# Two small products as one of 512 columns: reordering the LoRA part of a conditional residual kernel

## Chip, cores and metric

One core of a Trainium2 chip (trn2). The metric is the device time of one launch in microseconds, as a median of repeated runs.

## What is computed

For each of 8 batch elements, x is 512 tokens by 256 channels, fp32. Two residual layers follow each other. The first layer's weights are a mixture of 8 experts under one mask, by the element's 8 conditions; the second has a base matrix and 8 LoRA experts of rank 16, mixed by the same conditions:

```
# first layer
masked_w = weight * mask[None, :, :]
w_bot = jnp.einsum('bg,got->bot', y, masked_w)
x = x + jnp.einsum('bnt,bot->bno', x, w_bot) + bias
# second layer, scaling 2
out = jnp.einsum('btc,oc->bto', x, W_base) + b_base
h = jnp.einsum('btc,erc->bter', x, As)
lora = jnp.einsum('bter,eor,be->bto', h, Bs, w)
x = x + out + lora * SCALING
```

## The kernel before

The kernel folds both layers and both residuals into one 256x256 matrix per element: M = W0 W1, where W0 is identity plus the mixed and masked weights and W1 is identity plus base plus LoRA product. The output is M applied to x, plus a bias. All fp32 products are made of three matmuls of split operands: hi x hi, hi x lo and lo x hi, where `_hi` is a value rounded to fp32r and `_lo` what is left of it. So every operand has to be split, by two engines one behind the other: ScalarE writes `_hi` by a copy, then VectorE or GpSimd writes `_lo` by a subtraction.

The order is written out by hand, engine by engine, with semaphores between. On TensorE it is:

- 28 warm-up matmuls, then the LoRA products of elements 0 and 1 (`lora_first`).
- Mask products: `mixed(q)` for the 8 packs q = 0..7, each 4 matmuls of 128 columns. Pack q gives 32 of the 256 columns of the mixed weights of all 8 elements. They go to four PSUM banks in turn (`ps_mix`, which are the `ps_out` banks), so pack q from 4 on waits until VectorE took out pack q - 4. VectorE's `w0(q)` takes a pack out of PSUM, times the mask, into W0 and counts `w0_done`.
- LoRA products of elements 2 and 3 (`lora(b)`) between the mask products. `lora(b)` is two groups of three matmuls of 256 columns into bank b % 2 of `ps_lora`, and waits until VectorE took element b - 2 out. VectorE's `w1(b)` adds the base to it, giving W1 of the element.
- The first halves of the merges of elements 0 and 1, the LoRA products of 4 and 5 as a pair (`lora_pair`: 6 matmuls of 512 columns, bank j for row half j of both elements), then the second halves.
- For each element: merge of the next one, then apply (12 matmuls of 512 columns) of this one. The LoRA pair of 6 and 7 stands behind the third apply.

The first merges are split in halves so that they can start before all packs are in. Their first half needs a chain of its own: GpSimd splits W1 of element 0 (`w1_lo(0)`, line 191, after ScalarE's `w1_hi(0)`, line 240), adds the identity to the first half of W0 of elements 0 and 1 when four packs are in (line 206, `eye_first`), splits W1 of element 1, and, after ScalarE's `_hi` of W0 (line 286, `ramp_hi`), writes W0_lo of the first halves (line 210, `ramp_first`). In `merge_half`, this last is what the third of the three matmul pairs waits for (line 463), while line 580 holds the group until W1_lo is there. The second halves do the same by VectorE (lines 410 and 383) and ScalarE (line 295). `SINGLE` says how many elements have their LoRA product one at a time; waits on `lora_mm` and `w1_done` count by it. `W1BUF = 4` buffers hold W1.

GpSimd's order around the change is `w1_lo(0)`, identity, `w1_lo(1)`, W0_lo of the first halves, `w1_lo(2)`, and then a wait for VectorE's `x_lo` of element 0.

Of the kernel before, what the change touches and what calls it, by code (L numbers as in the profile page):

```python
# [5 lines left out]
def conditional_residual_kernel(nc: bass.Bass, head: bass.AP, rest: bass.AP, packs: bass.AP, factors_A: bass.AP,  # L6
# [10 lines left out]
    P = 128  # L17
    NB, _, XW = xT.shape
    NT = 2
# [9 lines left out]
    EXPW = KQ * C  # L29
    PACKW = EXPW + NT * TQ  # L30
    SCALING = 32.0 / 16
    SINGLE = 4
    XBUF = 4
    W1BUF = 4
    WARM = 28
# [5 lines left out]
    with ExitStack() as ctx:  # L41
# [40 lines left out]
        A_hi = sb("A_hi", [P, C], f32r)  # L82
        A_lo = sb("A_lo", [P, C], f32r)
        B_hi = sb("B_hi", [P, NB, C], f32r)
        B_lo = sb("B_lo", [P, NB, C], f32r)
# [20 lines left out]
        ps_lora = [pb(f"ps_lora{i}", [P, NT, C]) for i in range(2)]  # L106
# [17 lines left out]
        row_done, bias_mm, bias_done, bhi_done, blo_done = sem("row_done"), sem("bias_mm"), sem("bias_done"), sem("bhi_done"), sem("blo_done")  # L124
# [104 lines left out]
        @block.scalar  # L229
        def _(act):  # L230
            def b_hi(b):
                nc.scalar.activation(B_hi[:, b], B_er, ACT.Copy,
                                     scale=cond_er[:, b:b + 1]).then_inc(bhi_done, 1)

            def w1_hi(b):
                act.wait_ge(w1_done, b + 1 if b < SINGLE else b // 2 * 2 + 2)

                if b >= W1BUF:
                    act.wait_ge(merge_mm, b - W1BUF + 1)
                nc.scalar.activation(W1_hi[:, b % W1BUF], W1[:, b % W1BUF], ACT.Copy).then_inc(w1hi_done, 1)  # L240

            def w0_hi(b):

                act.wait_ge(eye_done, b - 1)
                act.wait_ge(merge_mm, b - 1)
                nc.scalar.activation(W0_hi[:, b % 2], W0[:, b], ACT.Copy).then_inc(w0hi_done, 1)  # L246

            def m_hi(b):
                act.wait_ge(merge_mm, b + 1)

                if b >= 2:
                    act.wait_ge(apply_mm, 2 * (b - 1))
                nc.scalar.activation(M_hi[:, b % 2], ps_merge[b % 2][:, :, :], ACT.Copy).then_inc(mhi_done, 1)  # L253

            def split_x_hi(b):
                act.wait_ge(x_in[b], 16)

                if b >= XBUF:
                    act.wait_ge(apply_mm, 2 * (b - XBUF + 1))
                nc.scalar.activation(x_hi[:, b % XBUF], x_sb[:, b], ACT.Copy).then_inc(xhi_done, 1)  # L260

            def out0(b):
                act.wait_ge(apply_mm, 2 * b + 1)
                if b == 0:
                    act.wait_ge(bias_done, 1)

                if b >= 2:
                    act.wait_ge(stored[b % 2][0], 16 * (b // 2))
                nc.scalar.activation(out_sb[:, b % 2, 0, :], ps_out[b % 2 * NT][:, :], ACT.Identity,  # L269
                                     bias=bias_sb[:, 0, b:b + 1]).then_inc(out_done[0], 1)  # L270

            act.dma_start(lora_sb[:, OBT:OBT + C], factors_B).then_inc(B_arrived, 16)

            act.wait_ge(warm_set, 1)
            nc.scalar.activation(table_sb[:, :], warm[:, 0:1], ACT.Copy)
            act.dma_start(base_sb[:, :, :], base.rearrange("p (j o) -> p j o", j=NT)).then_inc(base_in, 16)

            act.wait_ge(B_arrived, 16)
            act.wait_ge(lora_arrived, 16)
            for b in range(NB):  # L280
                b_hi(b)
            w1_hi(0)
            w1_hi(1)

            act.wait_ge(eye_first, 1)
            nc.scalar.activation(W0_hi[:, 0:2, :, 0:H], W0[:, 0:2, :, 0:H], ACT.Copy).then_inc(ramp_hi, 1)
            w1_hi(2)
            split_x_hi(0)

            act.wait_ge(rows_in, 16)  # L290
            act.wait_ge(w0_done, NQ)
            nc.scalar.activation(ps_row, bias0_row, ACT.Copy).then_inc(row_done, 1)
            for b in range(2):
                act.wait_ge(eye_second, 1)
                nc.scalar.activation(W0_hi[:, b, :, H:C], W0[:, b, :, H:C], ACT.Copy).then_inc(ramp_hi, 1)
            w1_hi(3)
            m_hi(0)
            split_x_hi(1)
            w0_hi(2)
            m_hi(1)  # L300
            for b in range(NB):
                if b + 3 < NB:
                    w0_hi(b + 3)
                if b + 2 < NB:
                    split_x_hi(b + 2)
                if 4 <= b + 3 < NB:
                    w1_hi(b + 3)
                if b + 2 < NB:
                    m_hi(b + 2)
                out0(b)  # L310

            b = NB - 1
            act.wait_ge(apply_mm, 2 * b + 2)
            act.wait_ge(stored[b % 2][1], 16 * (b // 2))
            nc.scalar.activation(out_sb[:, b % 2, 1, 0:TOK // 2], ps_out[b % 2 * NT + 1][:, 0:TOK // 2], ACT.Identity,
                                 bias=bias_sb[:, 1, b:b + 1]).then_inc(last_done, 1)

        @block.vector
        def _(dve):
# [8 lines left out]
            def w1(b):  # L328
                dve.wait_ge(lora_mm, b + 1)
                nc.vector.tensor_tensor(W1[:, b], ps_lora[b % 2][:, :, :], base_sb[:, :, :],  # L330
                                        ALU.add).then_inc(w1_done, 1)

            def w1_pair(b):
                dve.wait_ge(lora_mm, SINGLE + (b - SINGLE) // 2 + 1)
                dve.wait_ge(w1lo_done, b - W1BUF + 2)
                at = b % W1BUF
                for j in range(NT):
                    nc.vector.tensor_tensor(W1[:, at:at + 2, j, :], ps_lora[j][:, :, :],
                                            base_sb[:, j, :].unsqueeze(1).to_broadcast([P, 2, C]),
                                            ALU.add).then_inc(w1_done, 1)  # L340

            def w0(q):
                dve.wait_ge(mix_mm, q + 1)

                dve.wait_ge(pack_in[q], 16)
                ts = slice(q * TQ, (q + 1) * TQ)
                nc.vector.tensor_tensor(  # L347
                    W0[:, :, :, ts].rearrange("p b j t -> p j b t"),
                    ps_mix[q % 4][:, :].rearrange("p (j b t) -> p j b t", j=NT, t=TQ),
                    pack(q)[1].unsqueeze(2).to_broadcast([P, NT, NB, TQ]),  # L350
                    ALU.mult).then_inc(w0_done, 1)
# [43 lines left out]
            dve.wait_ge(fixed_done, 1)  # L395
            w0(0)
            w0(1)
            dve.wait_ge(base_done, NT)
            w1(0)
            w0(2)  # L400
            w1(1)
            w0(3)
            w0(4)
            w1(2)
            w0(5)
            w0(6)
            w1(3)
            w0(7)
            dve.wait_ge(w0_done, NQ)
            nc.vector.tensor_tensor(W0[:, 0:2, 1, H:C], W0[:, 0:2, 1, H:C], ident[:, :].unsqueeze(1).to_broadcast([P, 2, P]),  # L410
# [41 lines left out]
        def _(pe):  # L452
            def product(out, terms, lo_ready=None, mid_ready=None):


                for n, (hi_l, _, hi_r, _) in enumerate(terms):
                    nc.tensor.matmul(out, hi_l, hi_r, start=(n == 0), stop=False)  # L457
                if mid_ready is not None:
                    pe.wait_ge(*mid_ready)
                for hi_l, _, _, lo_r in terms:  # L460
                    nc.tensor.matmul(out, hi_l, lo_r, start=False, stop=False)  # L461
                if lo_ready is not None:
                    pe.wait_ge(*lo_ready)
                for n, (_, lo_l, hi_r, _) in enumerate(terms):
                    mm = nc.tensor.matmul(out, lo_l, hi_r, start=False, stop=(n == len(terms) - 1))  # L465
                return mm
# [23 lines left out]
                term(1, 1, A_lo, B_hi)  # L490
                term(1, 1, A_hi, B_lo, last=True).then_inc(lora_mm, 1)

            def lora(b):

                pe.wait_ge(blo_done, b + 1)
                pe.wait_ge(w1_done, b - 1)
                for j in range(NT):
                    cols = slice(j * P, (j + 1) * P)
                    mm = product(ps_lora[b % 2][:, j, :],
                                 [(A_hi[:, cols], A_lo[:, cols], B_hi[:, b], B_lo[:, b])])  # L500
                mm.then_inc(lora_mm, 1)

            def lora_pair(b):

                pe.wait_ge(blo_done, b + 2)
                pe.wait_ge(w1_done, b)
                both = slice(b, b + 2)
                for j in range(NT):
                    cols = slice(j * P, (j + 1) * P)
                    mm = product(ps_lora[j][:, :, :], [(A_hi[:, cols], A_lo[:, cols], B_hi[:, both], B_lo[:, both])])  # L510
                mm.then_inc(lora_mm, 1)
# [57 lines left out]
            lora_first()  # L569
            for q in range(4):  # L570
                mixed(q)
            lora(2)
            mixed(4)
            mixed(5)
            lora(3)
            mixed(6)
            mixed(7)
            for b in range(2):
# [75 lines left out]
```

## Time and profile before

| what | value |
|---|---|
| median of 3 runs | 56.79 us (56.75 to 57.19) |
| the profiled execution | 56.88 us |
| its span | 55.1 us |
| TensorE busy (matmuls) | 50.7 us, 92% |
| VectorE, ScalarE, GpSimd busy | 39.5, 31.7, 31.5 us |

The span runs from the first to the last instruction that the profile shows; the rest of the execution's time lies around it. PE is TensorE, PEld its weight loads, DVE VectorE, ACT ScalarE, POOL GpSimd. In a timeline a row gives the start, the duration of the whole group, the engine, line and operation, what it writes and reads, and in brackets the idle time of the engine before it with what ended it. Matmuls overlap: the next one starts before the one in front has ended, so TensorE's pace is read from start to start. Buffer numbers and the digits of W0 and W1 are left out in the names: W stands for both.

### The profile page before, as it was taken

The numbers are of one execution on the slowest core, as the hardware profiler recorded it, in microseconds if no ns is written. First come the engines' busy times: TensorE is split into PE (matmuls) and PEld (weight loads), VectorE is DVE, ScalarE is ACT, GpSimd is POOL, SyncE is SP. The second block draws the span as 40 slices with busy tenths as digits, with TensorE's granted clock in tenths as the row PEclk, the third lists the DMA queues.
The fourth block names the chain that finished last, engine by engine and source line by source line (L and its number), as shares of the span: only waits on it lengthen the run. The fifth ranks groups of instructions, "written<-read, shape, count | busy, mean of one in ns | idle before, by whom it ended". The sixth has DMA issues, their size and how long they took to land.

```text
span 55.1 us, 972 instructions
## 1 busy us (share of the span) xinstructions
PE 50.7 (92%) x330; PEld 45.6 (83%) x330; DVE 39.5 (72%) x64; ACT 31.7 (58%) x53; POOL 31.5 (57%) x30
## 2 busy tenths in 40 slices
PE   2998999699999999999999999999999999999900
PEld 2988999699998978998898889889889889888800
DVE  0049999989596975999999988689929809805030
ACT  1939900447809499619705992992992950850800
POOL 4003400199990098999995999999999910000000
PEclk9999999999999999999999999999999999999999
DMA  0599999999999995000630072063054054059582
GB/s 0 136 377 313 363 390 400 426 401 426 425 384 413 416 396 208 15 0 0 253 134 0 12 272 109 0 241 146 0 223 158 0 205 176 0 196 372 193 286 95
DMA packets 5477, 11.79 MB, mean 214 GB/s; under 512 B 609, under 2 KB 1377, under 8 KB 5473
## 3 DMA queue, kind: packets, MB, share of 16 engines
q1 hardware_dynamic: 5184, 11.35, 54.7%
q10 hardware_dynamic: 288, 0.39, 2.1%
q8 instruction: 2, 0.03, 0.2%
q14 instruction: 3, 0.02, 0.1%
HBM read 7.54 MB, written 4.19 MB: 213 GB/s over the span
## 4 chain that ended last, share of the span: by engine, by line
PE 77%; DVE 11%; DMA 5%; issue 2%; DVEq 0%
PE ps_out L457 13%; PE ps_out L461 13%; PE ps_out L465 13%; PE ps_merge L457 7%; PE ps_merge L461 7%; PE ps_merge L465 7%; DVE B_lo L324 7%; PE ps_out L527 6%; DMA lora_sb<-factors_A_dram 5%; PE ps_lora L457 3%; PE ps_lora L461 3%; PE ps_lora L465 3%; DVE W L330 1%; DVE out_sb L448 1%; DVE A_lo L389 1%
## 5 line engine op out<-in xcount | busy, mean ns | idle before, releaser
L191 POOL TENSOR_TENSOR W_lo<-W,W_hi 128x512 fp32r<-128x512 f32 x8 | 13.3, 1657 | 5.3 <-ACT W_hi L240 5.3
L358 DVE TENSOR_TENSOR x_lo<-x_sb,x_hi 128x1024 fp32r<-128x1024 f32 x8 | 11.9, 1485 | 0.2 <-ACT x_hi L260 0.2
L457 PE MATMUL ps_out<-x_hi,M_hi 128*128 128x512 f32 (+1 forms) x32 | 9.8, 388 | 0.0
L461 PE MATMUL ps_out<-x_lo,M_hi 128*128 128x512 f32 (+1 forms) x32 | 9.7, 384 | 0.0
L465 PE MATMUL ps_out<-x_hi,M_lo 128*128 128x512 f32 (+1 forms) x32 | 9.7, 383 | 0.0
L253 ACT ACTIVATE M_hi<-ps_merge 128x512 fp32r<-128x512 f32 x8 | 4.8, 595 | 7.6 <-PE ps_merge L465 7.6
L197 POOL TENSOR_TENSOR W_lo<-W,W_hi 128x512 fp32r<-128x512 f32 x6 | 8.8, 1459 | 0.3 <-ACT W_hi L246 0.3
L260 ACT ACTIVATE x_hi<-x_sb 128x1024 fp32r<-128x1024 f32 x8 | 8.4, 1055 | 0.0
L240 ACT ACTIVATE W_hi<-W 128x512 fp32r<-128x512 f32 x8 | 5.0, 629 | 5.9 <-DVE W L330 3.6
L373 DVE TENSOR_SCALAR out_sb<-ps_out,bias_sb 128x512 f32<-128x512 f32 x7 | 5.2, 747 | 4.1 <-PE ps_out L465 4.0
L201 POOL TENSOR_TENSOR W<-W,ident 128x256 f32<-128x256 f32 x6 | 6.4, 1071 | 2.9 <-DVE x_lo L358 2.9
L527 PE MATMUL ps_out<-packs_sb 128*128 128x128 f32 x64 | 7.6, 275 | 0.0
L527 PEld LDWEIGHTS ps_out<-packs_sb 128*128 128x128 f32 x64 | 7.4, 192 | 0.0
L461 PEld LDWEIGHTS ps_out<-x_lo,M_hi 128*128 128x128 f32 x32 | 5.9, 188 | 1.2
L465 PEld LDWEIGHTS ps_out<-x_hi,M_lo 128*128 128x128 f32 x32 | 5.9, 188 | 1.2
L365 DVE TENSOR_TENSOR M_lo<-ps_merge,M_hi 128x512 fp32r<-128x512 f32 x8 | 5.5, 687 | 2.0 <-ACT M_hi L253 1.9
L269 ACT ACTIVATE out_sb<-ps_out,bias_sb 128x512 f32<-128x512 f32 x8 | 5.5, 684 | 2.2 <-PE ps_out L465 2.2
L457 PE MATMUL ps_merge<-W_hi 128*128 128x256 f32 x32 | 6.6, 288 | 0.0
L461 PE MATMUL ps_merge<-W_lo,W_hi 128*128 128x256 f32 x32 | 6.4, 283 | 0.0
L465 PE MATMUL ps_merge<-W_hi,W_lo 128*128 128x256 f32 x32 | 6.4, 283 | 0.0
L457 PEld LDWEIGHTS ps_out<-x_hi,M_hi 128*128 128x128 f32 x32 | 5.5, 189 | 0.9 <-issue 0.2
L347 DVE TENSOR_TENSOR W<-ps_out,packs_sb 128x512 f32<-128x512 f32 x8 | 5.4, 686 | 0.9 <-PE ps_out L527 0.8
(58 smaller groups left out, 71.4 us busy)
## 6 DMA issues: line engine op xcount, KB each, us to landing
x_sb<-xT_dram SPq DMA_DIRECT2D x8, 512.0 KB, 10.5
outT_dram<-out_sb SPq DMA_DIRECT2D x15, 256.0 KB, 2.3
packs_sb<-packs_dram SPq DMA_DIRECT2D x7, 288.0 KB, 5.4
rows_sb<-rows_dram SPq DMA_DIRECT2D x1, 384.0 KB, 7.1
base_sb<-base_dram ACTq DMA_DIRECT2D x1, 256.0 KB, 3.6
outT_dram<-out_sb SPq DMA_DIRECT2D x2, 128.0 KB, 1.8
packs_sb<-head_dram SPq DMA_DIRECT2D x1, 192.0 KB, 3.5
packs_sb<-rest_dram SPq DMA_DIRECT2D x1, 160.0 KB, 3.9
```

The lines of the kernel that those rows point to most:

```text
L191: pool.tensor_tensor(W1_lo[:, b % W1BUF], W1[:, b % W1BUF], W1_hi[:, b % W1BUF].bitcast(f32), ALU.subtract).then_inc(w1lo_done, 1)
L197: pool.tensor_tensor(W0_lo[:, b % 2], W0[:, b], W0_hi[:, b % 2].bitcast(f32), ALU.subtract).then_inc(w0lo_done, 1)
L201: pool.tensor_tensor(diagonal(b), diagonal(b), ident[:, :].unsqueeze(1).to_broadcast([P, NT, P]), ALU.add).then_inc(eye_done, 1)
L260: nc.scalar.activation(x_hi[:, b % XBUF], x_sb[:, b], ACT.Copy).then_inc(xhi_done, 1)
L269: nc.scalar.activation(out_sb[:, b % 2, 0, :], ps_out[b % 2 * NT][:, :], ACT.Identity, bias=bias_sb[:, 0, b:b + 1]).then_inc(out_done[0], 1)
L347: nc.vector.tensor_tensor(W0[:, :, :, ts].rearrange("p b j t -> p j b t"), ps_mix[q % 4][:, :].rearrange("p (j b t) -> p j b t", j=NT, t=T ...
L358: nc.vector.tensor_tensor(x_lo[:, b % XBUF], x_sb[:, b], x_hi[:, b % XBUF].bitcast(f32), ALU.subtract).then_inc(xlo_done, 1)
L365: nc.vector.tensor_tensor(M_lo[:, b % 2], ps_merge[b % 2][:, :, :], M_hi[:, b % 2].bitcast(f32), ALU.subtract).then_inc(mlo_done, 1)
L457: nc.tensor.matmul(out, hi_l, hi_r, start=(n == 0), stop=False)
L461: nc.tensor.matmul(out, hi_l, lo_r, start=False, stop=False)
L465: mm = nc.tensor.matmul(out, lo_l, hi_r, start=False, stop=(n == len(terms) - 1))
L527: mm = nc.tensor.matmul(dst[:, j, :, k, :], pack(q)[0][:, k, j * P:(j + 1) * P], mix, start=True, stop=True)
```

## The change

The LoRA products of elements 2 and 3 are made as a pair of 512 columns, behind the sixth mask product (pack 5) where the first of them stood behind the fourth. VectorE takes W1 of elements 0 and 1 behind three mask products, the first of them one place later than before, and W1 of 2 and 3 in the broadcast form of `w1_pair`, behind W0 of pack 5. ScalarE splits x of element 0 ahead of W1 of element 2. `lora(b)` is gone.

```
--- before.py
+++ after.py
@@ -29,7 +29,7 @@
     EXPW = KQ * C
     PACKW = EXPW + NT * TQ
     SCALING = 32.0 / 16
-    SINGLE = 4
+    SINGLE = 2
     XBUF = 4
     W1BUF = 4
     WARM = 28
@@ -284,8 +284,8 @@
 
             act.wait_ge(eye_first, 1)
             nc.scalar.activation(W0_hi[:, 0:2, :, 0:H], W0[:, 0:2, :, 0:H], ACT.Copy).then_inc(ramp_hi, 1)
+            split_x_hi(0)
             w1_hi(2)
-            split_x_hi(0)
 
             act.wait_ge(rows_in, 16)
             act.wait_ge(w0_done, NQ)
@@ -332,7 +332,8 @@
 
             def w1_pair(b):
                 dve.wait_ge(lora_mm, SINGLE + (b - SINGLE) // 2 + 1)
-                dve.wait_ge(w1lo_done, b - W1BUF + 2)
+                if b >= W1BUF:
+                    dve.wait_ge(w1lo_done, b - W1BUF + 2)
                 at = b % W1BUF
                 for j in range(NT):
                     nc.vector.tensor_tensor(W1[:, at:at + 2, j, :], ps_lora[j][:, :, :],
@@ -395,16 +396,15 @@
             dve.wait_ge(fixed_done, 1)
             w0(0)
             w0(1)
+            w0(2)
             dve.wait_ge(base_done, NT)
             w1(0)
-            w0(2)
             w1(1)
             w0(3)
             w0(4)
-            w1(2)
             w0(5)
+            w1_pair(2)
             w0(6)
-            w1(3)
             w0(7)
             dve.wait_ge(w0_done, NQ)
             nc.vector.tensor_tensor(W0[:, 0:2, 1, H:C], W0[:, 0:2, 1, H:C], ident[:, :].unsqueeze(1).to_broadcast([P, 2, P]),
@@ -490,16 +490,6 @@
                 term(1, 1, A_lo, B_hi)
                 term(1, 1, A_hi, B_lo, last=True).then_inc(lora_mm, 1)
 
-            def lora(b):
-
-                pe.wait_ge(blo_done, b + 1)
-                pe.wait_ge(w1_done, b - 1)
-                for j in range(NT):
-                    cols = slice(j * P, (j + 1) * P)
-                    mm = product(ps_lora[b % 2][:, j, :],
-                                 [(A_hi[:, cols], A_lo[:, cols], B_hi[:, b], B_lo[:, b])])
-                mm.then_inc(lora_mm, 1)
-
             def lora_pair(b):
 
                 pe.wait_ge(blo_done, b + 2)
@@ -569,10 +559,9 @@
             lora_first()
             for q in range(4):
                 mixed(q)
-            lora(2)
             mixed(4)
             mixed(5)
-            lora(3)
+            lora_pair(2)
             mixed(6)
             mixed(7)
             for b in range(2):
```

VectorE, from its first mask product taken out to the identity add on the second halves (the order of before, then the order now; W0 rows are mask packs 0 to 7, W1 rows LoRA elements):

```order
L347 TENSOR_TENSOR W0<-ps_out0,packs_sb 128x2x8x32
L347 TENSOR_TENSOR W0<-ps_out1,packs_sb 128x2x8x32
L330 TENSOR_TENSOR W1<-ps_lora0,base_sb 128x512
L347 TENSOR_TENSOR W0<-ps_out2,packs_sb 128x2x8x32
L330 TENSOR_TENSOR W1<-ps_lora1,base_sb 128x512
L347 TENSOR_TENSOR W0<-ps_out3,packs_sb 128x2x8x32
L347 TENSOR_TENSOR W0<-ps_out0,packs_sb 128x2x8x32
L330 TENSOR_TENSOR W1<-ps_lora0,base_sb 128x512
L347 TENSOR_TENSOR W0<-ps_out1,packs_sb 128x2x8x32
L347 TENSOR_TENSOR W0<-ps_out2,packs_sb 128x2x8x32
L330 TENSOR_TENSOR W1<-ps_lora1,base_sb 128x512
L347 TENSOR_TENSOR W0<-ps_out3,packs_sb 128x2x8x32
```

Now, on the same engine and over the same place:

```order
L348 TENSOR_TENSOR W0<-ps_out0,packs_sb 128x2x8x32
L348 TENSOR_TENSOR W0<-ps_out1,packs_sb 128x2x8x32
L348 TENSOR_TENSOR W0<-ps_out2,packs_sb 128x2x8x32
L330 TENSOR_TENSOR W1<-ps_lora0,base_sb 128x512
L330 TENSOR_TENSOR W1<-ps_lora1,base_sb 128x512
L348 TENSOR_TENSOR W0<-ps_out3,packs_sb 128x2x8x32
L348 TENSOR_TENSOR W0<-ps_out0,packs_sb 128x2x8x32
L348 TENSOR_TENSOR W0<-ps_out1,packs_sb 128x2x8x32
L339 TENSOR_TENSOR W1<-ps_lora0,base_sb 128x2x256
L339 TENSOR_TENSOR W1<-ps_lora1,base_sb 128x2x256
L348 TENSOR_TENSOR W0<-ps_out2,packs_sb 128x2x8x32
L348 TENSOR_TENSOR W0<-ps_out3,packs_sb 128x2x8x32
```

W1 of element 0 went from third to fourth place, W1 of element 1 stayed fifth; the two of elements 2 and 3 stand together, and the last two packs follow them.

TensorE, from the mask product of pack 3 to the first merge, before (bank names tell the pack and the element):

```order
L527 MATMUL ps_out3<-packs_sb 128x8x16 x4
L457 MATMUL ps_lora0<-B_hi,A_hi 128x256
L461 MATMUL ps_lora0<-B_lo,A_hi 128x256
L465 MATMUL ps_lora0<-B_hi,A_lo 128x256
L457 MATMUL ps_lora0<-B_hi,A_hi 128x256
L461 MATMUL ps_lora0<-B_lo,A_hi 128x256
L465 MATMUL ps_lora0<-B_hi,A_lo 128x256
L527 MATMUL ps_out0<-packs_sb 128x8x16 x4
L527 MATMUL ps_out1<-packs_sb 128x8x16 x4
```

And TensorE now, from the same product on:

```order
L517 MATMUL ps_out3<-packs_sb 128x8x16 x4
L517 MATMUL ps_out0<-packs_sb 128x8x16 x4
L517 MATMUL ps_out1<-packs_sb 128x8x16 x4
L457 MATMUL ps_lora0<-B_hi,A_hi 128x512
L461 MATMUL ps_lora0<-B_lo,A_hi 128x512
L465 MATMUL ps_lora0<-B_hi,A_lo 128x512
L457 MATMUL ps_lora1<-B_hi,A_hi 128x512
L461 MATMUL ps_lora1<-B_lo,A_hi 128x512
L465 MATMUL ps_lora1<-B_hi,A_lo 128x512
L517 MATMUL ps_out2<-packs_sb 128x8x16 x4
```

The mask products of packs 4 and 5 moved ahead of the LoRA products, and the group that stood between packs 5 and 6 (the other six of 256 columns) is now part of the pair there.

## Rows read from the trace of the kernel before

**Rows 1.** The page: busy time, granted clock, chain that ended last.

```profile
PE 50.7 (92%) x330; PEld 45.6 (83%) x330; DVE 39.5 (72%) x64; ACT 31.7 (58%) x53; POOL 31.5 (57%) x30
...
PEclk9999999999999999999999999999999999999999
...
PE 77%; DVE 11%; DMA 5%; issue 2%; DVEq 0%
```

**Rows 2.** Timeline of PE; start us, us, engine, line, operation [idle before].

```profile
5.96 3.73 PE L527 MATMUL ps_out<-packs_sb 128*128 128x128 f32 x32
10.15 0.36 PE L457 MATMUL ps_lora<-B_hi,A_hi 128*128 128x256 f32 x1 [0.45 <-DVE W L330]
...
10.94 1.95 PE L527 MATMUL ps_out<-packs_sb 128*128 128x128 f32 x16
...
13.44 1.95 PE L527 MATMUL ps_out<-packs_sb 128*128 128x128 f32 x16
15.13 0.48 PE L457 MATMUL ps_merge<-W_hi 128*128 128x256 f32 x2
...
15.69 0.40 PE L465 MATMUL ps_merge<-W_hi,W_lo 128*128 128x256 f32 x2
...
16.65 0.40 PE L457 MATMUL ps_lora<-B_hi,A_hi 128*128 128x512 f32 x1
...
18.04 0.40 PE L457 MATMUL ps_merge<-W_hi 128*128 128x256 f32 x2
```

**Rows 3.** Timeline of DVE, 8.1 to 16.9 us.

```profile
8.12 1.29 DVE L347 TENSOR_TENSOR W<-ps_out,packs_sb 128x512 f32<-128x512 f32 x2
9.32 0.68 DVE L330 TENSOR_TENSOR W<-ps_lora,base_sb 128x512 f32<-128x512 f32 x1
9.92 0.68 DVE L347 TENSOR_TENSOR W<-ps_out,packs_sb 128x512 f32<-128x512 f32 x1
10.52 0.68 DVE L330 TENSOR_TENSOR W<-ps_lora,base_sb 128x512 f32<-128x512 f32 x1
11.11 0.68 DVE L347 TENSOR_TENSOR W<-ps_out,packs_sb 128x512 f32<-128x512 f32 x1
...
15.73 0.68 DVE L347 TENSOR_TENSOR W<-ps_out,packs_sb 128x512 f32<-128x512 f32 x1
16.45 0.43 DVE L410 TENSOR_TENSOR W<-W,ident 128x256 f32<-128x256 f32 x1
```

**Rows 4.** Timeline of ACT, 10 to 15 us.

```profile
10.04 0.63 ACT L240 ACTIVATE W_hi<-W 128x512 fp32r<-128x512 f32 x1 [3.02 <-DVE W L330]
...
12.74 0.63 ACT L286 ACTIVATE W_hi<-W 128x512 fp32r<-128x512 f32 x1 [0.88 <-POOL W L206]
...
13.89 1.04 ACT L260 ACTIVATE x_hi<-x_sb 128x1024 fp32r<-128x1024 f32 x1
```

**Rows 5.** Timeline of POOL, 10.7 to 15.2 us.

```profile
10.75 1.28 POOL L191 TENSOR_TENSOR W_lo<-W,W_hi 128x512 fp32r<-128x512 f32 x1 [4.60 <-ACT W_hi L240]
11.98 0.73 POOL L206 TENSOR_TENSOR W<-W,ident 128x256 f32<-128x256 f32 x1
12.67 1.30 POOL L191 TENSOR_TENSOR W_lo<-W,W_hi 128x512 fp32r<-128x512 f32 x1
13.92 1.28 POOL L210 TENSOR_TENSOR W_lo<-W,W_hi 128x512 fp32r<-128x512 f32 x1
```

**Rows 6.** Timelines of POOL, then DVE, where the two meet later.

```profile
25.29 1.30 POOL L197 TENSOR_TENSOR W_lo<-W,W_hi 128x512 fp32r<-128x512 f32 x1
...
28.24 1.30 POOL L197 TENSOR_TENSOR W_lo<-W,W_hi 128x512 fp32r<-128x512 f32 x1
30.22 2.20 POOL L191 TENSOR_TENSOR W_lo<-W,W_hi 128x512 fp32r<-128x512 f32 x1 [0.68 <-ACT W_hi L240]
...
25.50 2.18 DVE L358 TENSOR_TENSOR x_lo<-x_sb,x_hi 128x1024 fp32r<-128x1024 f32 x1
...
28.20 1.27 DVE L338 TENSOR_TENSOR W<-ps_lora,base_sb 128x512 f32<-128x512 f32 x2
```

More of the change, by code:

```diff
@@ L31, in conditional_residual_kernel @@
     SCALING = 32.0 / 16
-    SINGLE = 4
+    SINGLE = 2
     XBUF = 4
@@ L286, in _ @@
             nc.scalar.activation(W0_hi[:, 0:2, :, 0:H], W0[:, 0:2, :, 0:H], ACT.Copy).then_inc(ramp_hi, 1)
+            split_x_hi(0)
             w1_hi(2)
-            split_x_hi(0)
             act.wait_ge(rows_in, 16)
@@ L334, in w1_pair @@
                 dve.wait_ge(lora_mm, SINGLE + (b - SINGLE) // 2 + 1)
-                dve.wait_ge(w1lo_done, b - W1BUF + 2)
+                if b >= W1BUF:
+                    dve.wait_ge(w1lo_done, b - W1BUF + 2)
                 at = b % W1BUF
@@ L397, in _ @@
             w0(1)
+            w0(2)
             dve.wait_ge(base_done, NT)
             w1(0)
-            w0(2)
             w1(1)
@@ L403, in _ @@
             w0(4)
-            w1(2)
             w0(5)
+            w1_pair(2)
             w0(6)
-            w1(3)
             w0(7)
@@ L491, in lora_first @@
                 term(1, 1, A_hi, B_lo, last=True).then_inc(lora_mm, 1)
[L493 to L501, printed above, removed]
             def lora_pair(b):
@@ L571, in _ @@
                 mixed(q)
-            lora(2)
             mixed(4)
             mixed(5)
-            lora(3)
+            lora_pair(2)
             mixed(6)
```

## The prediction

> **What bounds the kernel now.** I read the page first. TensorE is busy for 50.7 of 55.1 us, its granted clock is at 9 (full, the 2.4 GHz level) in every slice, and the chain that ended last is TensorE for 77%, with VectorE at 11% ahead of it [rows 1]. So only two things can move the end: a pause of TensorE, or the number and length of its instructions. The next view is TensorE's own timeline [rows 2]. The reader is to see one pause behind the mask products: those of packs 0 to 3 end at 9.69 (5.96 + 3.73), and the third LoRA product starts at 10.15, 0.46 later, released by VectorE's W1. From there on it goes from one group to the next. VectorE's timeline [rows 3] says why: W1 of element 0 runs from 9.32 to 10.00, and the LoRA product follows 0.14 later (rounded starts and ends; every sum here is good to some 0.02).
>
> Then I look for what stands just behind TensorE, since a pause that goes only pays up to the next thing that is late. That is the first half of the first two merges. It starts at 15.13 and its third pair of matmuls (W0_lo) at 15.69 [rows 2]. Its inputs come by a second chain: VectorE W1(0) [rows 3], ScalarE W1_hi(0) at 10.04 [rows 4], then four GpSimd instructions: W1_lo(0) at 10.75, identity into W0 at 11.98, W1_lo(1) at 12.67, and W0_lo of the first halves from 13.92 to 15.20 [rows 5]. The first of them waits for ScalarE, the other three have no idle time noted before them. So GpSimd is a full chain of 4.45 us from 10.75 to 15.20, and is only 0.49 us ahead of TensorE's use at 15.69. That margin decides this case.
>
> **The change part by part.**
>
> 1. *TensorE's LoRA products.* Removed: 12 matmuls of 256 columns in two groups; the first takes 0.79 from its start to the next group (10.15 to 10.94) [rows 2]. Added: 6 of 512 columns. The same shape runs at 16.65, and its six take 1.39 (to 18.04) [rows 2]. Behind mask products the first matmul costs some 0.07 more (0.79 for six where six of the 0.12 pitch would be 0.72), so 1.46 against 2 x 0.79 = 1.58: a gain of 0.12 on TensorE's own time.
>
> 2. *The pause at 9.69 goes, since the mask products of packs 4 and 5 now follow at once.* Mask products go at (3.73 - 0.28) / 31 = 0.111 each, so packs 0 to 3 give way at 5.96 + 32 x 0.111 = 9.52. They need W0 of packs 0 and 1 taken out (VectorE is done with both at 9.41 [rows 3]) and packs 4 and 5 landed; the DMA view bounds that poorly, but this term is shown below to have 0.9 us of cover. Sixteen mask products take 15.13 - 13.44 = 1.69 [rows 2], which gives 11.21. The pair then waits for W1 of elements 0 and 1. VectorE writes the second at 10.52 to 11.20 in both kernels, plus the 0.14: 11.34. Six matmuls: 12.80. Packs 6 and 7: 14.49. TensorE so reaches the merges 0.64 ahead of the 15.13 of before, and the W0_lo pair, 0.56 further on, at 15.05 in place of 15.69.
>
> 3. *VectorE takes W0 of pack 2 ahead of W1(0).* The pitch is 0.60 (9.32, 9.92, 10.52) [rows 3]. The product of pack 2 is finished at 5.96 + 23 x 0.111 + 0.28 = 8.8, so this instruction starts at 9.32 without a wait, and W1(0) runs at 9.92 to 10.60: 0.60 later. W1(1) stays at 10.52 and W0 of pack 3 at 11.11, as five instructions stand ahead of the latter either way.
>
> 4. *What waits behind W1(0).* ScalarE's W1_hi(0) is the head of its queue, so it moves from 10.04 to 10.64. GpSimd's W1_lo(0) moves from 10.75 to 11.35. By the same pitches the other three go to 12.58, 13.27 and 14.52, and W0_lo ends at 15.80. Their other inputs come no later: the identity wants four W0 (11.11 + 0.68 = 11.79), W1_lo(1) wants W1_hi(1) (from 11.20, a 0.63 instruction), and W0_lo wants ScalarE's W0_hi, which moves with the identity from 12.74 to 13.34 and ends at 13.97, well ahead of 14.52 [rows 4]. So this chain is 0.60 late, and its margin was 0.49. TensorE gets there at 15.05, waits until 15.80, and starts at 15.94 if the step from GpSimd costs what VectorE's did, 0.14. Against 15.69 that is **+0.25 us**. The trace has no case of TensorE waiting for GpSimd. The nearest steps are 0.04 (W1 to ScalarE, 10.00 to 10.04) and 0.14 to 0.21 (VectorE to TensorE, with the slow first matmul of 0.07), so the term lies between +0.15 and +0.32; I take 0.14 since it is the same waiting engine.
>
> 5. *W1 of elements 2 and 3 in two broadcast instructions.* Same number, and the same form costs 1.27 for two at 28.20 [rows 6] where the old ones were 0.68 each. They are ready at 12.96 and run from 13.02; W0 of pack 6 then starts at 14.22 and of pack 7 at 14.82, where it was 15.73. The identity add on VectorE comes at 15.54 in place of 16.45 [rows 3]. Cost nothing: TensorE wants the second halves of W0_hi and W0_lo only from 18.04 [rows 2]. Likewise W1_hi(2) behind x_hi(0) on ScalarE: x has landed by 13.89 [rows 4], ScalarE gets there at 13.97, and W1_lo(2) is first used in the third merge, after 22 us. If that cover went, a late x would hold up W1_hi(2) and the bias row, which TensorE needs for none of the first merges. The second LoRA pair, at 16.65, wants W1 of elements 2 and 3, done by 14.3.
>
> 6. *GpSimd beside VectorE.* Now VectorE's identity add (15.54, two operands in SBUF) meets the last 0.26 us of GpSimd's W0_lo (to 15.80). Such a meeting stands in the trace: GpSimd started at 25.29 and took 1.30, its usual time, while VectorE's x_lo, issued at 25.50, took 2.18 [rows 6]. The one that came second paid. So W0_lo keeps 15.80 and VectorE's add ends at 15.80 + 0.43 = 16.23, still ahead of the 16.88 of before. Were the meeting shared out instead, W0_lo could lose up to the add's 0.43 and the time would be 57.47. The Trainium skill (SBUF — State Buffer, SBUF: two separate sides) says that a VectorE instruction with two SBUF inputs and a GpSimd instruction take one shared port pair as an exclusive lock, the first to start holding it for its whole length; by that rule GpSimd's chain isn't touched and the sum stays, and the rows at 25.29 and 25.50 agree.
>
> The sum: TensorE's 0.12 and the 0.46 pause are gained ahead of 15 us and handed back as a new wait of 0.89 (15.05 to 15.94). What is left is +0.25. Behind the merges TensorE has no wait that could take this up again, and ScalarE, VectorE and GpSimd are released there by TensorE's merges, so they move along. Span 55.10 + 0.25 = 55.35, and the profiled execution 56.88 + 0.25 = 57.13. The median of the three runs before stands 0.09 below the profiled one, so the forecast is 56.79 + 0.25 = **57.04 us**. What measurement can tell here is about 1%, 0.57 us.
>
> **The rivals.**
>
> A, *the head start is kept.* If GpSimd's chain doesn't hold TensorE, it comes 0.64 early: 56.15. For it: spans on GpSimd are rough, and TensorE never waited there before. Against: three of four instructions stand back to back, and VectorE's order makes the head of the chain 0.60 late whatever its end is. To keep half of the gain W0_lo would have had to be done by 14.6, 0.6 ahead of its record.
>
> B, *a wash.* If GpSimd's real end lies 0.2 ahead of its record, the shift is about +0.05: 56.84. This is still within 1%.
>
> C, *slower.* One of GpSimd's four instructions, W1_lo(1) or W0_lo, at 13.27 to 15.80, is caught by VectorE and takes the long form, 2.20 as at 30.22 where it met an x_lo, not 1.28 [rows 5, 6]: 0.92 more, 57.96. It decides from about 0.32 us of such delay on. For it: VectorE now runs the broadcast form at 13.02 to 14.22, which stood there never before. Against: the same form at 28.20 ran beside a GpSimd instruction of 1.30 at 28.24 [rows 6], and it has one operand in PSUM as all others in that stretch have. By the rule of the Trainium skill named above, with only one SBUF input it takes no lock, and C would not occur.
>
> D, *the change doesn't do what it says*, the LoRA pair waiting elsewhere. The printed orders speak against it, and its own cover is 0.9 us: packs late by that much change nothing.
>
> **How the numbers follow.** My forecast (with +0.15 to +0.32) has 0.75, B 0.10, A 0.04, C or the shared meeting 0.08 (of which half falls short of 1%), D and the rest 0.03. The range is 56.6 to 57.5: below, B and 0.24 more, about half the spread of 0.44 of the three times before; above, the shared meeting. A and C stay outside. Faster by over 1%: A and little else, 0.04. Slower by over 1%, beyond 57.36: part of C and of the step's upper bound, 0.08. Within 1%: 0.88.
>
> **What would show it.** In the profile after: no idle time of TensorE at 9.7; W1(0) on VectorE at 9.92; GpSimd's W0_lo from 14.5 to 15.8; idle time of 0.9 us on TensorE before the first W0_lo matmul, released by GpSimd; first product of the first apply 0.25 later than before. It is wrong if that wait is absent or under 0.6, if W1(0) isn't 0.6 late, if a GpSimd instruction in that stretch takes over 1.5 us, or if the clock row falls after the pause.

## The result and the profile after

The changed kernel takes 57.09 us (median of 10 runs, 57.02 to 57.53) where the kernel before takes 56.82 beside it: ratio 1.0053, 95% interval 1.003 to 1.0077. Forecast were +0.25 us and 57.04 us; measured are +0.27 us and 57.09 us. It is a small loss: its interval lies above no change, and its size inside the 1% that the prediction took as what measurement can tell.

The first profile of the changed kernel (one execution of 57.36 us, span 55.6) answers to [rows 2] to [rows 5], but not at the times forecast. TensorE's timeline, columns as in [rows 2]:

```profile
4.99 0.41 PE L471 MATMUL ps_lora<-B_hi,A_lo 128*128 128x256 f32 x1
5.20 0.41 PE L471 MATMUL ps_lora<-B_lo,A_hi 128*128 128x256 f32 x1
...
6.66 2.62 PE L517 MATMUL ps_out<-packs_sb 128*128 128x128 f32 x22
...
11.93 0.48 PE L457 MATMUL ps_lora<-B_hi,A_hi 128*128 128x512 f32 x1
...
15.11 0.48 PE L457 MATMUL ps_merge<-W_hi 128*128 128x256 f32 x2
...
16.09 0.50 PE L465 MATMUL ps_merge<-W_hi,W_lo 128*128 128x256 f32 x2 [0.27 <-POOL W_lo L210]
16.43 0.40 PE L457 MATMUL ps_merge<-W_hi 128*128 128x256 f32 x2
```

The kernel before, in the same place of TensorE's timeline:

```profile
5.01 0.28 PE L471 MATMUL ps_lora<-B_lo,A_hi 128*128 128x256 f32 x1
5.12 0.28 PE L471 MATMUL ps_lora<-B_hi,A_hi 128*128 128x256 f32 x1
```

VectorE's timeline of the changed kernel's execution:

```profile
9.53 0.69 DVE L348 TENSOR_TENSOR W<-ps_out,packs_sb 128x512 f32<-128x512 f32 x1 [0.20 <-PE ps_out L517]
10.14 1.28 DVE L330 TENSOR_TENSOR W<-ps_lora,base_sb 128x512 f32<-128x512 f32 x2
...
16.12 1.44 DVE L410 TENSOR_TENSOR W<-W,ident 128x256 f32<-128x256 f32 x1
```

And GpSimd's:

```profile
11.56 1.29 POOL L191 TENSOR_TENSOR W_lo<-W,W_hi 128x512 fp32r<-128x512 f32 x1 [4.39 <-ACT W_hi L240]
12.81 0.74 POOL L206 TENSOR_TENSOR W<-W,ident 128x256 f32<-128x256 f32 x1
13.52 1.27 POOL L191 TENSOR_TENSOR W_lo<-W,W_hi 128x512 fp32r<-128x512 f32 x1
14.75 1.29 POOL L210 TENSOR_TENSOR W_lo<-W,W_hi 128x512 fp32r<-128x512 f32 x1
15.99 1.29 POOL L191 TENSOR_TENSOR W_lo<-W,W_hi 128x512 fp32r<-128x512 f32 x1
```

The signs that were forecast are there: no idle time of TensorE at 9.7, and a new one before the first W0_lo product, released by GpSimd's line 210. But TensorE is late. In the LoRA products at its head one matmul follows the other every 0.21 us (4.99, 5.20), where it was some 0.12 before (5.01, 5.12); below this distance from start to start is called the pitch. The mask products begin at 6.66, not at 5.96 [rows 2]. (The x22 of their row is where that view ends; all go on to 11.93.) So TensorE idles only 0.27 at the merges, and VectorE's W0 of pack 2 has to wait 0.20 for its mask product. The prediction had named an idle time under 0.6 as a sign that it is wrong, and this profile shows that sign. Whether the late TensorE belongs to the change is the question of the eighth experiment.

### The profile page after: what moved, and what is told of

Its sections match the earlier page's. It is cut to its first block, busy times and chain, and to the rows that moved or that the text cites. A ratio compares the mean times of both kernels' runs of the same rounds, so it can differ in the third digit from the quotient of the medians.

```text
span 55.6 us, 959 instructions
## 1 busy us (share of the span) xinstructions
PE 51.5 (93%) x324; PEld 46.1 (83%) x324; DVE 40.8 (74%) x64; ACT 31.6 (57%) x53; POOL 31.5 (57%) x30
## 4 chain that ended last, share of the span: by engine, by line
PE 81%; POOL 8%; DVE 2%; issue 2%; ACT 1%; DVEq 0%
PE ps_out L457 13%; PE ps_out L461 13%; PE ps_out L465 13%; PE ps_merge L465 7%; PE ps_merge L457 7%; PE ps_merge L461 6%; PE ps_merge L558 6%; PE ps_out L517 5%; PE ps_lora L471 5%; POOL W_lo L191 5%; POOL W_lo L210 2%; PE ps_lora L457 2%; PE ps_lora L465 2%; PE ps_lora L461 2%; POOL W L206 1%
## 5 line engine op out<-in xcount | busy, mean ns | idle before, releaser
L457 PEld LDWEIGHTS ps_merge<-W_hi 128*128 128x128 f32 x32 | 5.2, 190 | 0.6
```

## The experiments

Theory: TensorE's head start is real, but the first W0_lo product waits for GpSimd's chain, whose head W1(0) the change made 0.60 later. Rivals: the LoRA pair and its place cost the time; or VectorE's order costs nothing. The first four ran together, then the next four, then three, each group beside runs of the kernel before. e10 and e11 are single profiled executions and so not in the table; "the ramp" is all that stands ahead of the first apply.

| kernel | median us | before beside it | ratio (95% interval) |
|---|---|---|---|
| e1 W1(0) back | 56.73 | 56.85 | 0.9979 (0.9949 to 1.0008) |
| e2 VectorE's order alone | 57.43 | 56.85 | 1.0087 (1.0062 to 1.0113) |
| e3 GpSimd +0.6, before | 57.07 | 56.85 | 1.0041 (1.0024 to 1.0059) |
| e4 GpSimd +0.6, changed | 57.65 | 56.85 | 1.0127 (1.0103 to 1.0152) |
| e5 identity on VectorE | 56.88 | 56.84 | 1.0003 (0.9972 to 1.0033) |
| e6 ScalarE's order undone | 57.18 | 56.84 | 1.0066 (1.0037 to 1.0094) |
| e7 place without pair | 56.54 | 56.84 | 0.9961 (0.9929 to 0.9992) |
| e8 changed kernel again | 57.14 | 56.84 | 1.0064 (1.0029 to 1.0098) |
| e9 as e7, again | 56.68 | 56.86 | 0.9968 (0.9942 to 0.9994) |

**e1, from the changed kernel.**

```
-            w0(2)
             dve.wait_ge(base_done, NT)
             w1(0)
+            w0(2)
             w1(1)
```

> The changed kernel with one line moved: VectorE takes W1 of element 0 behind two mask packs again, as before the change; the LoRA pair stays. Theory (GpSimd's chain, whose head is W1(0), holds the first W0_lo product): W1(0) ends at about 10.0, W0_lo on GpSimd at about 15.2, TensorE reaches its use early, at about 15.05, and starts it at about 15.3, 0.35 earlier than in the kernel before (15.69). Time 56.82 - 0.35 = 56.47 us, 0.6 below the changed kernel. Rival (the pair and its place cost the time): no gain from the line, 57.1 us.

The line alone takes the loss away: 56.73 is 0.36 below the changed kernel's 57.09. The quickest five executions of twelve lie at 56.47 to 56.53, at the forecast; the others go up to 57.47. The interval of e1 still touches no change against the kernel before. Its profile came from an execution of 56.95 us, with the pitch of 0.21: W0_lo on GpSimd ends at 13.83 + 1.30 = 15.13, and TensorE, which came to it only at 15.64, doesn't wait:

```profile
6.64 5.52 PE L517 MATMUL ps_out<-packs_sb 128*128 128x128 f32 x48
...
15.64 0.40 PE L465 MATMUL ps_merge<-W_hi,W_lo 128*128 128x256 f32 x2
```

In this execution the limit has changed sides: GpSimd is done 0.51 ahead of TensorE's use. The wait of under 0.3 that the theory has for the quick executions was not seen, as the second profile of this kernel (e11, 56.90 us) had the pitch of 0.21 once more.

> The kernel with W1(0) behind two packs and the pair kept, once more, for a profile with the pitch of 0.12. Theory: GpSimd's W0_lo ends at 15.1 to 15.2 and TensorE starts its product 0.05 later with a wait of under 0.3 us; time 56.5 us. Rival: TensorE waits at the mask packs before, and not for GpSimd.

**e2, from the kernel before:** the reverse of e1's edit, with single LoRA products.

> The kernel before with only VectorE's order changed: W0 of pack 2 ahead of W1(0), LoRA products one by one as before. Theory: W1(0) is 0.60 later, the third LoRA product waits until 10.75 in place of 10.15, and everything of TensorE behind it goes 0.60 later: 57.4 us; GpSimd's chain (0.60 later too, with 0.49 to spare) is then hidden behind TensorE's own delay. Rival (the order on VectorE costs nothing): 56.8 us. So the LoRA pair would be worth 0.3 us in the changed kernel.

57.43 against 57.4 forecast. The third LoRA product starts at 10.85, 0.70 later than in the kernel before, released by VectorE's W1:

```profile
10.85 0.36 PE L457 MATMUL ps_lora<-B_hi,A_hi 128*128 128x256 f32 x1 [0.58 <-DVE W L330]
```

VectorE's order costs 0.6 us by itself, and the rest of the change (the new place of the LoRA products, and the pair) gives 0.3 of it back.

**e3 and e4: a dose for GpSimd,** in the kernel before and in the changed one.

```
             w1_lo(0)
+            pool.tensor_tensor(spare[:, :, :], ident[:, :].unsqueeze(1).to_broadcast([P, 2, P]),
+                               ident[:, :].unsqueeze(1).to_broadcast([P, 2, P]), ALU.add)
             pool.wait_ge(w0_done, NQ // 2)
```

(The line that makes the unused tile `spare` is left out.)

> The kernel before with one extra GpSimd instruction of 256 columns (0.7 us, into an unused tile) behind the split of W1(0). Theory: the chain had 0.49 less the step of 0.04 to 0.14 to spare, so of 0.70 some 0.3 shows: 57.15 us. Rival (GpSimd had ample room): 56.8 us.

> The changed kernel with the same extra GpSimd instruction of 0.7 us. Theory: the chain is what TensorE waits for, so all of it shows: 57.1 + 0.7 = 57.8 us. Rival (the loss is elsewhere and GpSimd's wait is hidden): under 57.4 us.

The instruction moved its successor by 0.57 us (12.41 to 12.98 in e4). The kernel before lost 0.22 and the changed one 0.56 (57.65 against 57.09, which ran in another group). So the changed kernel has no room left on GpSimd, and the one before had some 0.35. e4's profile shows the wait at its full size and the step from GpSimd to TensorE, 14.92 + 1.28 = 16.20 to 16.25:

```profile
14.43 0.50 PE L460 MATMUL ps_merge<-W_hi 128*128 128x256 f32 x2
14.77 0.40 PE L464 MATMUL ps_merge<-W_lo,W_hi 128*128 128x256 f32 x2
16.25 0.50 PE L468 MATMUL ps_merge<-W_hi,W_lo 128*128 128x256 f32 x2 [1.07 <-POOL W_lo L213]
```

and on GpSimd's timeline:

```profile
14.92 1.28 POOL L213 TENSOR_TENSOR W_lo<-W,W_hi 128x512 fp32r<-128x512 f32 x1
```

**e6: the changed kernel with `w1_hi(2)` ahead of `split_x_hi(0)` again.**

> The changed kernel with ScalarE's order put back: W1 of element 2 ahead of x of element 0. ScalarE then waits for the pair's W1 until 14.3 and does x_hi(0) behind it, up to 1 us later. Theory (ScalarE's order costs and gains nothing, as its outputs are first used after 17 us): 57.1 us, as the changed kernel. Rival (the swap was a part of the result): over 57.3 us, if TensorE's second merge halves or x come late.

57.18 us and a ratio of 1.0066, against 1.0064 of e8 beside it: no effect. Its profile (57.10 us) is the cleanest view of what was forecast, as its LoRA matmuls have the pitch of 0.12:

```profile
5.90 5.63 PE L517 MATMUL ps_out<-packs_sb 128*128 128x128 f32 x48
11.29 0.47 PE L457 MATMUL ps_lora<-B_hi,A_hi 128*128 128x512 f32 x1
...
14.46 0.48 PE L457 MATMUL ps_merge<-W_hi 128*128 128x256 f32 x2
14.78 0.40 PE L461 MATMUL ps_merge<-W_lo,W_hi 128*128 128x256 f32 x2
15.81 0.51 PE L465 MATMUL ps_merge<-W_hi,W_lo 128*128 128x256 f32 x2 [0.63 <-POOL W_lo L210]
16.15 0.40 PE L457 MATMUL ps_merge<-W_hi 128*128 128x256 f32 x2
```

and GpSimd's instruction that it waits for:

```profile
14.47 1.29 POOL L210 TENSOR_TENSOR W_lo<-W,W_hi 128x512 fp32r<-128x512 f32 x1
```

**e7 and e9: the kernel before with the place alone.** LoRA products stay single; W1(0) stays behind two packs.

```
-            lora(2)
             mixed(4)
             mixed(5)
+            lora(2)
             lora(3)
...
             w0(4)
-            w1(2)
             w0(5)
-            w0(6)
+            w1(2)
             w1(3)
+            w0(6)
             w0(7)
```

> The kernel before with both later LoRA products moved behind the mask product of pack 5, but still one by one with 256 columns, and VectorE's W1 of elements 0 and 1 in their old places. Theory: the place removes the pause and GpSimd's chain stays the limit, so the time is that of the first experiment, 56.5 to 56.7 us; the broadcast pair form itself is worth at most 0.1. Rival (the 512-column form is what gains): 56.8 us or more.

> The kernel that keeps single LoRA products, both behind pack 5, once more, since its interval touched that of no change. Theory: it beats the kernel before in executions whose first LoRA matmuls have the pitch of 0.12, by 0.3 us (56.5), and not in those with 0.21, where TensorE itself comes 0.6 late; median 56.6 us. Rival (the gain was chance): 56.8 us.

In both groups it is faster than the kernel before, by 0.30 and 0.18 us (0.4% and 0.3%), with both intervals below 1. This is the version that beats both kernels. It is no slower than e1, so the 512-column form isn't what gains. The two profiles show what the pitch does here. e9's, of 56.64 us, has five matmuls at 0.21. TensorE comes to the W0_lo product 0.21 earlier than in the kernel before and finds it ready:

```profile
6.44 5.52 PE L527 MATMUL ps_out<-packs_sb 128*128 128x128 f32 x48
...
15.48 0.40 PE L465 MATMUL ps_merge<-W_hi,W_lo 128*128 128x256 f32 x2
```

as GpSimd's part ends at 13.95 + 1.28 = 15.23:

```profile
13.95 1.28 POOL L210 TENSOR_TENSOR W_lo<-W,W_hi 128x512 fp32r<-128x512 f32 x1
```

e7's, of 57.18 us, has some eleven matmuls at 0.21: the mask products begin at 6.94 and the W0_lo product at 15.99, 0.30 later than in the kernel before, and the execution is 0.30 us longer than the profiled one of before. So e9's theory (no gain where the pitch is 0.21) was right for e7's execution and wrong for e9's own: how many matmuls are slow decides.

**e8: the changed kernel once more.**

> The changed kernel itself, for a second look. In its first profile the first seven LoRA matmuls had a pitch of 0.21 us and the mask products began at 6.66; in the kernel before it was 0.12 and 5.96. Theory: in an execution with the pitch of 0.12 TensorE reaches the first W0_lo product at about 15.0 and waits until about 15.8 to 15.9; in one with 0.21 it comes at 15.6 and waits until 16.1. Time 57.1 us. Rival (the 0.6 us later arrival at 15.6 belongs to the change): the arrival stays at 15.6 with the pitch of 0.12 too.

57.14 us. In its profile (57.08 us) three matmuls have the pitch of 0.21 and the mask products begin at 6.17. TensorE comes to the merges at 14.61 and so to the product at about 15.17, and GpSimd lets it go at 15.77:

```profile
6.17 5.52 PE L517 MATMUL ps_out<-packs_sb 128*128 128x128 f32 x48
...
14.61 0.48 PE L457 MATMUL ps_merge<-W_hi 128*128 128x256 f32 x2
...
15.77 0.50 PE L465 MATMUL ps_merge<-W_hi,W_lo 128*128 128x256 f32 x2 [0.44 <-POOL W_lo L210]
16.11 0.40 PE L457 MATMUL ps_merge<-W_hi 128*128 128x256 f32 x2
```

So the late arrival of the first profile wasn't the change's: it goes with the number of slow LoRA matmuls at the head. The profile of the kernel before with e3's dose had some ten of them, and its mask products began at 6.78. The idle time is again under the prediction's 0.6; from start to start the wait is 15.77 - 15.17 = 0.60.

**e5 and e10: from e1, the identity add (`eye_first`) taken from GpSimd and given to VectorE behind `w0(3)`.**

```
             w1_lo(0)
-            pool.wait_ge(w0_done, NQ // 2)
-            pool.tensor_tensor(W0[:, 0:2, 0, 0:H], W0[:, 0:2, 0, 0:H], ident[:, :].unsqueeze(1).to_broadcast([P, 2, P]),
-                               ALU.add).then_inc(eye_first, 1)
             w1_lo(1)
...
             w0(3)
+            dve.wait_ge(w0_done, NQ // 2)
+            nc.vector.tensor_tensor(W0[:, 0:2, 0, 0:H], W0[:, 0:2, 0, 0:H], ident[:, :].unsqueeze(1).to_broadcast([P, 2, P]),
+                                    ALU.add).then_inc(eye_first, 1)
             w0(4)
```

> The kernel of the first experiment (W1(0) behind two packs, LoRA pair kept) with the identity add on the first halves of W0 moved from GpSimd to VectorE, behind W0 of pack 3. Theory: GpSimd's chain loses one of its four links (0.7 us), less what VectorE's add takes from it while both want SBUF (up to 0.4), so W0_lo ends at about 14.85 and TensorE, at its use at about 15.03, no longer waits: 0.64 ahead of the kernel before, 56.2 us, 0.2 to 0.3 below the first experiment's quick executions. VectorE's own later work moves by up to 0.7 us and has that room. Rival (the first experiment's W0_lo wasn't the last to come any more, or VectorE's delay of W1 of elements 2 and 3 decides): 56.5 us or more.

> The kernel with the identity add on VectorE once more, for a profile of an execution with the pitch of 0.12, since its time (56.7 at best) missed the 56.2 that was expected. Theory: VectorE's add, issued at about 11.6, is held by GpSimd's W1_lo(0) until 11.94 and, if GpSimd's next one then comes first, until 13.2; the packs and the pair's W1 behind it on VectorE come up to 1.2 us late and TensorE waits there. Rival: TensorE waits for mask packs to land, at 8 to 11 us, in any kernel that wants them earlier, and the add has no part in it.

56.88 us (56.66 at best), where 56.2 was expected: a miss. e5's own profile (57.25 us) has the pitch of 0.21 for some eleven matmuls; e10's (56.72 us) has the short pitch. There the first part went as forecast: the W0_lo product starts at 15.09 without a wait, 0.60 earlier than before, and the first apply at 19.16, 0.49 earlier. Neither the theory of e10 nor its rival holds: VectorE's add took 0.47 at 11.76, held up by almost nothing. Most of the lead is lost at the fifth merge (element 4). TensorE's timeline of e10:

```profile
31.71 0.39 PE L461 MATMUL ps_lora<-B_lo,A_hi 128*128 128x512 f32 x1
31.94 0.39 PE L465 MATMUL ps_lora<-B_hi,A_lo 128*128 128x512 f32 x1
32.38 0.47 PE L457 MATMUL ps_merge<-W_hi 128*128 128x256 f32 x2
```

and GpSimd's:

```profile
28.09 1.29 POOL L197 TENSOR_TENSOR W_lo<-W,W_hi 128x512 fp32r<-128x512 f32 x1
30.07 2.21 POOL L191 TENSOR_TENSOR W_lo<-W,W_hi 128x512 fp32r<-128x512 f32 x1 [0.69 <-ACT W_hi L237]
```

The pitch of 0.23 becomes 0.44 ahead of that merge. It waits for W1_lo of element 4, and GpSimd's record of it ends at 30.07 + 2.21 = 32.28, 0.10 earlier. Its 2.21 is the long form, beside VectorE's x_lo at 29.91. In the kernel before, the same merge started at 32.65 and the W1_lo had ended at 30.22 + 2.20 = 32.42 [rows 6]:

```profile
32.65 0.40 PE L457 MATMUL ps_merge<-W_hi 128*128 128x256 f32 x2
```

The other profiles bear this out. In e1, e5 and e11 too, the merge starts 0.10 behind the end of that record and the pitch ahead of it is stretched. In the kernel before and in e9 it starts 0.23 behind, with no stretch, so the kernel before had some 0.13 to spare there. TensorE was 0.48 ahead of the kernel before at the LoRA products (30.81 and 31.29), but the W1_lo only 0.14 (32.28 and 32.42); at the apply behind the merge 0.20 of the lead is left (33.88 and 34.08). No run moved that W1_lo by itself, so this is read from profiles and not tested.

The profiles also hint at a price of the pair. In e1, e10 and e11 GpSimd waits 0.48 to 0.74 for W1_hi of element 2, for which it doesn't wait in e9, and splits W1 of element 2 at 15.37 to 15.61 (e9: 15.19). VectorE's identity add on the second halves comes while this split runs and takes 1.08 to 1.09 us, against 0.84 in e9 and 0.43 in the kernel before. x_lo of element 0 comes behind it on VectorE, at 18.11 in e10 and 17.93 in e9. e11 is 0.10 ahead of the kernel before at 31.19 and 0.01 behind it at the apply at 34.09; e9 carries its 0.22 through whole (31.07 and 33.87). No run was made to separate this.

## Why the prediction was right, point by point

- *TensorE's part (steps 1 and 2).* With the short pitch, as in e6: pair at 11.29 (forecast 11.34), merges at 14.46 (14.49), use of W0_lo 0.56 behind it, 15.02 (15.05). The 1.46 and 1.69 of the sum were 1.47 and 1.70 in e6 and e8.
- *VectorE and GpSimd (steps 3 and 4).* W1(0) starts at 9.87 in e6 (forecast 9.92) and W0_lo ends at 15.76 (15.80). The first apply starts at 19.86 there, 0.21 later than the 19.65 of the kernel before (0.25 forecast). e2 measured the order alone at 0.6, e3 and e4 the margin: gone in the changed kernel, some 0.35 in the one before, which is the 0.49 less the 0.15 of the step.
- *The step from GpSimd to TensorE* was made up otherwise, and that it came out right is luck. It took 0.05 (15.76 to 15.81 in e6), not the 0.14 borrowed from VectorE. But the pair of matmuls behind the wait takes 0.34 to the next one (15.81 to 16.15) in place of 0.24. Together 0.15: two wrong parts with the right sum, so that the second merge's products start at 16.15 in e6, where the working gives 16.18.
- *The wait* was forecast at 0.89 from start to start. It was 0.79 in e6; the idle time in the row, 0.63, is shorter, as the matmuls in front still run. In the two profiles of the changed kernel the idle time was 0.27 and 0.44, under the 0.6 that was to show the prediction wrong. The time came out right all the same, because GpSimd's end decides it: a TensorE that comes later waits less. The sign had taken TensorE's arrival as fixed, and the slow LoRA matmuls move it.
- *Not in the sum:* VectorE's W0 of pack 2 now stands ahead of W1(0), so W1(0) hangs on the third mask product. Where TensorE's head is slow, that is 0.20 late (9.53), and GpSimd's chain with it. Step 3 had called this free, for the product ends at 8.8; it does so only with the short pitch. In the first profile the W0_lo product starts 0.28 later than in e6 (16.09 and 15.81), and the execution took 0.26 longer (57.36 and 57.10). That the other slower executions of the changed kernel are of this kind isn't shown.
- *VectorE against GpSimd (step 6).* The order of arrival decided each time. In e6 the identity add came at 15.48 while GpSimd's W0_lo ran to 15.76, and took 0.56; in the first profile it came at 16.12, behind the start of GpSimd's next at 15.99, and took 1.44. The GpSimd instruction that had started first stayed at 1.29 both times; in e6 its next one, from 15.71, came behind VectorE's add and took 1.47. The rule of the Trainium skill (SBUF — State Buffer, SBUF: two separate sides), an exclusive lock for the first to start, agrees with these rows. W0_lo, for which TensorE waits, lost nothing by it, so rival C and the shared meeting fall.
- *Rivals A, B and D.* A falls by e4. B (GpSimd's real end 0.2 ahead of its record) falls by the step: TensorE starts 0.05 behind the record's end in e4, e6 and both profiles of the changed kernel. D falls by the orders of the rows. *ScalarE's part (step 5)* was free (e6). The pair's was free as far as the forecast goes: in the changed kernel's profiles the merge of element 4 isn't held. In e1 it may cost some 0.1 us, as said above.

What remains open: e1's interval touches no change, so that a gain over the kernel before rests on e7 and e9, which share its VectorE order for W1(0). And no profile shows one of the quick executions at 56.5 us: in those of e1, e7, e9 and e11 TensorE comes to the W0_lo product at 15.48 to 15.99, later than the 15.05 forecast, and doesn't wait for GpSimd. That GpSimd's chain is what holds the quick ones is worked out from rows, and not seen.

## What to carry to other kernels

Before removing a pause, look one wait further: here 0.46 us of pause stood ahead of a chain with 0.49 us to spare, and an edit that took 0.60 from that chain to win the pause turned a gain of 0.2 to 0.3 us (e7, e9) into a loss of 0.27. Where two chains meet, keep the head of the one without idle time where it is (W1(0)) and move the work of the other (the LoRA products); that version is the only one whose interval lies below no change. And a lead won early counts only up to the next thing that is just in time.

## What the runs showed that was not expected

TensorE's first LoRA matmuls of 256 columns go at one of two pitches, 0.21 and 0.12 us, and change from the first to the second after none to some eleven of them, in one kernel from one execution to the next. In the profiles it shifts the start of the mask products between 5.8 and 6.9 us. The row of the granted clock says full speed throughout in the profiles of both kernels (9 in every slice, 1.00 from 4.2 to 6.3 us). The two pitches lie near what 256 columns at one per clock would take at the two levels of the clock, 256 / 1.2 GHz = 0.213 and 256 / 2.4 GHz = 0.107 us. By this estimate a clock at its lower level that the row misses would fit, but no record shows it and no run was made to test it, so the cause stays open.

A kernel whose ramp is bound by TensorE pays for it: the version of e7 and e9 took 56.64 us with five slow matmuls and 57.18 with eleven. The changed kernel, bound by GpSimd, pays less: 57.10 with none (e6, with ScalarE's old order), 57.08 with three (e8), 57.36 with nine. The pitch is known for profiled executions only, so the spread of the others isn't explained by this.
